# The second half's router and its gate reads earlier, and two more pairs of layer 2 in row halves

## The reference, cut to what matters

```
logits = xt @ Wr + br
top_p, top_idx = top_k(softmax(logits), 2)
weights = top_p / top_p.sum(-1)
h = gelu(einsum('end,edh->enh', xe, W1) + b1)      # 8 experts, 64 -> 256
y = einsum('enh,ehd->end', h, W2) + b2             # 256 -> 64
out = t + sum of the two selected y, times their weights
```

## Time and profile before

| | us |
|---|---|
| time, median of 3 runs | 60.36 (59.89 to 60.62) |
| the profiled execution, its own time | 60.38 |
| its span | 58.5 |
| PE busy in it | 49.7 (85%) |
| DVE busy | 42.3 (72%) |
| ACT busy | 35.2 (60%) |
| POOL busy | 24.9 (42%) |

### The profile page before, as it was taken

One profiled execution on the slowest core, in us unless ns is written; L12 is line 12 of the kernel. 1 busy time (PEld: TensorE's weight loads), 2 busy tenths in 40 slices (PEclk: granted clock), 3 DMA queues, 4 the chain that ended last, 5 costly groups with the idle time before them and its releaser, 6 DMA issues.

```text
span 58.5 us, 1641 instructions
## 1 busy us (share of the span) xinstructions
PE 49.7 (85%) x556; PEld 29.1 (50%) x556; DVE 42.3 (72%) x175; ACT 35.2 (60%) x79; POOL 24.9 (42%) x49
## 2 busy tenths in 40 slices
PE   1997999999789999999999999995499999776420
PEld 0332847887647887654536445362246632052410
DVE  2198689697998988992600999999997409995630
ACT  5501459970958699798896978969708982000000
POOL 6239770000099899765099900298080000026000
PEclk9999999999999999999999999999999999999985
DMA  0351446983000000000000467601559600020012
GB/s 0 105 106 25 113 114 193 349 282 112 1 17 0 0 0 0 11 0 6 0 11 17 126 184 189 210 20 71 195 207 214 207 18 0 29 61 0 0 32 57
DMA packets 4584, 4.80 MB, mean 82 GB/s; under 512 B 2204, under 2 KB 3040, under 8 KB 4576
## 3 DMA queue, kind: packets, MB, share of 16 engines
q1 hardware_dynamic: 4256, 4.67, 26.6%
q10 hardware_dynamic: 320, 0.03, 0.6%
HBM read 4.41 MB, written 0.29 MB: 80 GB/s over the span
## 4 chain that ended last, share of the span: by engine, by line
PE 47%; DVE 16%; DMA 15%; issue 9%; SPq 7%; POOL 1%; ACT 1%; ACTq 0%; DVEq 0%; POOLq 0%
PE banks L1046 13%; PE banks L1074 9%; DMA G<-gates_kept 8%; SPq L312 6%; PE banks L980 4%; PE banks L1027 4%; PE banks L953 3%; DVE HG L746 3%; DMA X<-in_x_dram 3%; PE banks L1116 3%; DMA gates_kept<-gateT 3%; PE banks L932 2%; DVE PTS L602 2%; PE banks L1130 2%; PE banks L916 2%
## 5 line engine op out<-in xcount | busy, mean ns | idle before, releaser
L480 ACT ACTIVATE H<-banks,PF 128x512 f32<-128x512 f32 x32 | 19.6, 685 | 2.1 <-PE banks L1046 1.4
L1046 PE MATMUL banks<-XE,W1F 64*64 64x256 f32 x224 | 14.2, 380 | 0.1
L373 POOL TENSOR_TENSOR acc<-acc,gated 128x512 f32<-128x512 f32 x4 | 5.5, 1386 | 14.3 <-DVE gated L739 8.4
L1046 PEld LDWEIGHTS banks<-XE,W1F 64*64 64x64 f32 x224 | 8.5, 133 | 5.3 <-issue 3.3
L1074 PE MATMUL banks<-H,W2F 64*64 64x512 f32 x80 | 9.6, 594 | 1.5 <-issue 1.5
L356 POOL TENSOR_SCALAR XE<-XF,PF,LB 128x256 f32<-128x256 f32 x14 | 7.7, 564 | 2.2 <-ACT XF L458 2.2
L725 DVE TENSOR_TENSOR YS<-banks,YA 128x512 f32<-128x512 f32 x5 | 3.4, 689 | 4.7 <-ACT YA L490 4.4
L334 POOL TENSOR_TENSOR rs<-base,half 128x2 f32<-128x2 f32 x4 | 2.8, 701 | 8.6 <-DVE base L638 8.4
L916 PE MATMUL banks<-zeros 128*128 128x512 f16 x13 | 5.2, 534 | 1.3 <-POOL zeros L375 1.3
L1074 PEld LDWEIGHTS banks<-H,W2F 64*64 64x64 f32 x80 | 2.9, 132 | 5.2 <-issue 4.8
L490 ACT ACTIVATE YA<-banks,B2T 128x512 f32<-128x512 f32 x5 | 3.4, 687 | 3.1 <-PE banks L1074 3.1
(11 more groups left out here) (93 smaller groups left out, 80.2 us busy)
## 6 DMA issues: line engine op xcount, KB each, us to landing
GS<-gates_kept SPq DMA_DIRECT2D x14, 128.0 KB, 2.9
W1F<-in_w_dram SPq DMA_DIRECT2D x1, 768.0 KB, 4.9
W2F<-in_w_dram SPq DMA_DIRECT2D x1, 512.0 KB, 5.6
G<-gates_kept SPq DMA_DIRECT2D x2, 256.0 KB, 4.1
W1F<-in_w_dram SPq DMA_DIRECT2D x1, 256.0 KB, 3.3
out_dram<-res SPq DMA_DIRECT2D x4, 64.0 KB, 1.6
X<-in_x_dram SPq DMA_DIRECT2D x2, 64.0 KB, 2.0
X<-in_x_dram SPq DMA_DIRECT2D x1, 128.0 KB, 2.4
```

What stands on the lines that cost most here:

```text
L373: nc.gpsimd.tensor_tensor(acc[h][:, :], acc[h][:, :], gated[s % 2][:, :], ALU.add).then_inc(acc_ready, 1)
L480: nc.scalar.activation(H[:, r, :].rearrange("p (t n) -> p t n", t=PT), ps_z[z_slot(g // J)][:, :, PIX * j:PIX * j + PIX], ACT.Gelu, bias=P ...
L1046: mm = nc.tensor.matmul(ps_z[z_slot(q)][C * c:C * c + C, k, PIX * j:PIX * j + PIX], W1F[rows, e, j, C * c:C * c + C], XE[h][rows, e, :], s ...
```

## The change

- `SPLIT` is 7: steps 5 and 6 take the split form too (`layer2` is gone). For each of them a `keep_part` on ACT and a `sum_parts` on DVE are added, and `weigh` reads `YS` and `GS` in place of a bank.
- PE: `turn_gates(0)` and `turn_x2(3)` come ahead of `layer1(5)`; `logits(1)` goes from behind `layer1(7)` to ahead of `layer1(6)`; `turn_gates(1)` from behind `layer1(10)` to behind `layer1(7)`; `layer2_split(5)` comes ahead of `layer1(15)`, and `fold_sum` behind `layer2_split(6)`.
- ACT: `turn_gates(0)` and `turn_x2(3)` come ahead of `gelu(10)`, `tanh(1)` and `turn_gates(1)` further ahead as well.
- DVE: `route(1, 0)` and `route(1, 1)` come ahead of `sum_parts(0)`, all the other stages of `route(1)` ahead of `sum_parts(1)`, both `last_bias` between `sum_parts(1)` and `sum_parts(2)`; near the end `weigh_last(0)` and `(1)` stand ahead of `sum_parts(5)`, and the finish of half 0 stands behind `weigh(6)`.
- SP: the gates of half 1 are written out behind the reads of steps 0 and 1; then come the reads of steps 2 and 3, then those of step 7, and then steps 4 to 6.

```diff
-SPLIT = 5
+SPLIT = 7
 def sums_done(s):
-    return 4 * min(s + 1, SPLIT) + 2 * max(s + 1 - SPLIT, 0)
+    return 4 * (s + 1)
...
+            keep_gates(0)
+            spread_pair(0)
+            spread_pair(1)
+            keep_gates(1)
+            spread_pair(2)
+            spread_pair(3)
+            spread_last()
+            for s in range(PAIRS, STEPS - 1):
+                spread_pair(s)
...  (ACT)
             keep_part(0)
-            gelu(10)
             turn_gates(0)
             turn_x2(3)
-            for g in range(11, 14):
-                gelu(g)
-            keep_part(1)
-            for g in range(14, 17):
+            for g in range(10, 13):
                 gelu(g)
             tanh(1)
-            gelu(17)
+            gelu(13)
+            keep_part(1)
+            gelu(14)
+            turn_gates(1)
+            for g in range(15, 18):
+                gelu(g)
             keep_part(2)
...
-            for g in range(26, HALVES * UNITS):
+            for g in range(26, 30):
                 gelu(g)
+            keep_part(5)
+            gelu(30)
+            gelu(31)
+            keep_part(6)
...  (DVE, sum_parts and weigh)
-                if s == 4:
-                    dve.wait_ge(gated_ready, 1)
+                if s >= 4:
+                    dve.wait_ge(gated_ready, s - 3)
...
-                if s < SPLIT:
-                    dve.wait_ge(ysum_ready, s + 1)
-                    nc.vector.tensor_tensor(dst[:, :], YS[s % 4][:, :], GS[s][:, :], ALU.mult)...
-                else:
-                    dve.wait_ge(y_ps, sums_done(s))
-                    nc.vector.scalar_tensor_tensor(out=dst[:, :], in0=ps_y[s % 2], scalar=B2T[:, p:p + 1],
-                                                   in1=GS[s][:, :], op0=ALU.add, op1=ALU.mult)...
+                dve.wait_ge(ysum_ready, s + 1)
+                nc.vector.tensor_tensor(dst[:, :], YS[s % 4][:, :], GS[s][:, :], ALU.mult)...
...  (DVE, order; route(1, 0) and route(1, 1) ahead)
-            sum_parts(1)
+            sum_parts(0)
             for stage in range(2, 11):
                 route(1, stage)
+            sum_parts(1)
+            last_bias(0)
+            last_bias(1)
             sum_parts(2)
             weigh(0)
             weigh(1)
             weigh(2)
-            last_bias(0)
             sum_parts(3)
             weigh(3)
-            last_bias(1)
             sum_parts(4)
             weigh(4)
             weigh_last(0)
             weigh_last(1)
+            sum_parts(5)
+            weigh(5)
+            weigh_last(2)
+            weigh_last(3)
+            sum_parts(6)
+            weigh(6)
             finish_part()
             finish_first()
-            weigh_last(2)
-            weigh_last(3)
-            weigh(5)
-            weigh(6)
             add_third()
...  (PE, order)
             layer2_split(0)
-            layer1(5)
             turn_gates(0)
             turn_x2(3)
+            layer1(5)
+            logits(1)
             layer1(6)
             layer2_split(1)
             layer1(7)
-            logits(1)
+            turn_gates(1)
             layer1(8)
             layer2_split(2)
             layer1(9)
             layer1(10)
-            turn_gates(1)
             layer2_split(3)
             layer1(11)
             layer1(12)
             layer2_split(4)
             layer1(13)
             layer1(14)
+            layer2_split(5)
+            layer1(15)
+            layer2_split(6)
             fold_sum()
-            layer1(15)
-            layer2(5)
-            layer2(6)
             layer2_last(0)
             layer2_last(1)
```

More of the change, by code:

```diff
@@ L99, in build_block @@
         ps_part = [banks[:, 4 + r, :] for r in range(2)]
-        ps_y = [banks[:, 4 + k, :] for k in range(2)]
         ps_b2 = banks[:, 3, 0:PAIRS]
@@ L298, in _, with keep_gates, spread_pair, spread_last @@
             sp.dma_start(B2R[:, :, :], b2[0, E - 2:E, :].partition_broadcast(P)).then_inc(b2r_in, 16)
-            for s in range(STEPS):
-                h, p = s // PAIRS, s % PAIRS
[L302 to L306, removed]
-                for k in range(2):
-                    if s == STEPS - 1:
-                        sp.dma_start(G7[:, k, :], gates_kept[h, 2 * p + k, :].partition_broadcast(P)).then_inc(g7_in, 16)
-                    else:
-                        sp.dma_start(GS[s][C * k:C * k + C, :], gates_kept[h, 2 * p + k, :].partition_broadcast(C))\
-                            .then_inc(gates_in[s], 16)
+            def keep_gates(h):
+                sp.wait_ge(gateT_ready, h + 1)
+                sp.dma_start(gates_kept[h, :, :].rearrange("e (t n) -> t e n", t=TILES), gateT[h][:, :])\
+                    .then_inc(gates_out[h], 16)
+            def spread_pair(s):
+                h, p = s // PAIRS, s % PAIRS
+                sp.wait_ge(gates_out[h], 16)
+                for k in range(2):
+                    sp.dma_start(GS[s][C * k:C * k + C, :], gates_kept[h, 2 * p + k, :].partition_broadcast(C))\
+                        .then_inc(gates_in[s], 16)
+            def spread_last():
+                sp.wait_ge(gates_out[1], 16)
+                for k in range(2):
+                    sp.dma_start(G7[:, k, :], gates_kept[1, E - 2 + k, :].partition_broadcast(P)).then_inc(g7_in, 16)
+            keep_gates(0)
[7 more added lines that the diff above has]
+                spread_pair(s)
             for n in range(0, TILES, PT):
@@ L527, in _ @@
             keep_part(0)
-            gelu(10)
             turn_gates(0)
             turn_x2(3)
-            for g in range(11, 14):
-                gelu(g)
-            keep_part(1)
-            for g in range(14, 17):
+            for g in range(10, 13):
                 gelu(g)
             tanh(1)
-            gelu(17)
-            keep_part(2)
-            gelu(18)
-            gelu(19)
-            turn_gates(1)
-            gelu(20)
-            gelu(21)
+            gelu(13)
[4 more added lines that the diff above has]
+                gelu(g)
+            keep_part(2)
+            for g in range(18, 22):
+                gelu(g)
             keep_part(3)
@@ L733, in weigh @@
                 dst = acc[h] if p == 0 else gated[s % 2]
-                if s < SPLIT:
-                    dve.wait_ge(ysum_ready, s + 1)
-                    nc.vector.tensor_tensor(dst[:, :], YS[s % 4][:, :], GS[s][:, :], ALU.mult).then_inc(gated_ready, 1)
-                else:
-                    dve.wait_ge(y_ps, sums_done(s))
-                    nc.vector.scalar_tensor_tensor(out=dst[:, :], in0=ps_y[s % 2], scalar=B2T[:, p:p + 1],
-                                                   in1=GS[s][:, :], op0=ALU.add, op1=ALU.mult).then_inc(gated_ready, 1)
+                dve.wait_ge(ysum_ready, s + 1)
+                nc.vector.tensor_tensor(dst[:, :], YS[s % 4][:, :], GS[s][:, :], ALU.mult).then_inc(gated_ready, 1)
             def weigh_last(n):
@@ L881, in _ @@
             second_norm(3)
-            sum_parts(0)
             route(1, 0)
             route(1, 1)
-            sum_parts(1)
+            sum_parts(0)
             for stage in range(2, 11):
                 route(1, stage)
+            sum_parts(1)
+            last_bias(0)
+            last_bias(1)
             sum_parts(2)
@@ L1078, in layer2_split @@
                                 mm.then_inc(y_ps, 1)
[L1080 to L1091, removed]
             def turn_b2():
```

## The result

The change makes the kernel slower: 61.56 us (median of 4 runs, 60.91 to 61.78) against 60.12, a ratio of 1.0245 (95% interval 1.0124 to 1.0367). Run again, unaltered, on another occasion it gave 61.54 against 60.46, ratio 1.0203 (1.0142 to 1.0264). So it is slower; whether by more than 2% the intervals leave open. The forecast of 60.4 with a range to 61.0 was wrong.

A forecast was written before the change was run, and what follows sets the result against it. The prediction took step 7's gate reads, a last_bias/POOL collision and DVE's end as bounds; 1.49 and 0.77 of holes went on about 1.3 of router, 0.9 of idle and a longer tail: 60.38 + 0.06 = 60.4 us, range 59.1 to 61.0.

The forecast's parts named there:

- The path now: Products wait for step 7's reads (0.77 idle); last_bias meets POOL's additions, 1.49 idle ahead of layer2_split(4).
- The gate reads and last_bias: Step 7's DMA wait goes, moved gate writing costs nothing; eight last_bias instructions take 1.7 to 2.2 us, hidden.
- The router: POOL's stretches hold seven two-input DVE instructions; gate ends at 33.0, layer2_split(2) starts at 34.2 (32.89 before).
- The round of the banks: Split layer 2 round of 3.62 us, level with PE's work; PE idles about 0.9 between steps 5 and 6.
- The tail: From layer2_split(6)'s start to add_third 4.98 us, and the 0.73 wait for POOL's add_up(5) goes.
- rival C: At the end add_up(5) on POOL gets in ahead of product 2, rest 0.3 later; 60.8 (60.5 to 61.2), chance 0.13.
- B: Rival: router's small DVE instructions are not caught by POOL's stretches; 59.5 us (59.0 to 59.9), chance 0.22.
- D: Rival: PE's clock falls before L1130, its 1.08 us doubles, 61.5; chance 0.04. Elsewhere D: layer2_split(0)'s start to span's end.
- E: Rival: the holes close further than seen, for instance a round shorter than 3.62; below 59.0 us, chance 0.06.
- The sum: layer2_split(2) at 34.2 puts add_third at 53.66 against 53.60, total 60.38 + 0.06 = 60.4 us.
- The count from 60.38: Starting point: the profiled execution's 60.38 us, taken as equivalent to the median of three runs, 60.36.

The follow-up runs named there:

- g7_first: Kernel before, with SP issuing the two reads of step 7 ahead of those of steps 4 to 6: 59.26 us, ratio 0.9820.
- bias_ahead: Kernel before with step 7's reads ahead of those of steps 4 to 6 and both last_bias between sum_parts(2) and weigh(0): 57.94 us, ratio 0.9680.
- router_off_path: Changed kernel with turn_gates(1) behind layer2_split(2) on PE, keep_part(2) on ACT, sum_parts(1) between stages 7 and 8 of route(1): 61.12 us, ratio 1.0117.
- router_off_reads: router_off_path with SP issuing the reads of steps 2 and 3 ahead of the writing of half 1's gates: 59.90 us, ratio 0.9880.
- stretch_behind: Changed kernel with POOL waiting for half 1's gates before seven of the eight stretches: 59.99 us in a single execution (kernel before 60.24).
- finish_ahead: Changed kernel with fold_sum ahead of layer2_split(6) and the finish of half 0 ahead of weigh_last(2): 61.84 us, ratio 1.0197.

## Why the prediction was wrong, point by point

The forecast failed in three places: two terms of its sum were too small, the router's (by 0.22) and the tail's (by 0.29), and it was counted from one execution that had started early. The points follow its own order.

- **The path now.** Right: g7_first shows the DMA wait (1.34 of D), bias_ahead the collision of `last_bias` (a further 1.20).
- **The gate reads and last_bias.** Right. The products start without a DMA wait, L768 takes 1.86, and there is no idle ahead of `layer2_split(4)`. That moving the writing of the gates ahead of two steps of reads costs "nothing" held only because the gates were early: router_off_path shows 2.45 of wait once they are not.
- **The router.** The mechanism was right, and it is the largest single cost of the front (1.05, router_off_reads and stretch_behind). The term was 0.22 short: `layer2_split(2)` at 9.14, not 8.92. I had counted LG and gate among the caught, which slipped through at 0.19 each, and not the cast (0.50) and wab (0.53 for two), which have one input in SBUF each. wab ends at 33.23, where a stretch ends at 33.21. I had quoted the Trainium skill (SBUF — State Buffer, Who interferes with whom) only in half: its sentence on at most one SBUF input holds outside the two-port modes, and the same section names `copy`, `cast` and `tensor_scalar` among those that can enter such a mode and contend. The trace agrees that they are held, 0.50 beside a stretch and 0.17 without; in which mode they ran no row shows.
- **The round of the banks.** Right: 3.62, 3.65, 3.63, 3.63 against 3.62, and an idle of 0.82 between steps 5 and 6 against 0.9.
- **The tail.** Among the terms of the sum this step failed most: "From S6: 2.06 to `keep_part(6)`, 0.78 to `sum_parts(6)`, 0.61 to `weigh(6)`", in all 4.98. It was 5.27. `weigh(6)` starts 0.81 behind `sum_parts(6)`, not 0.61, because it waits for that very sum's semaphore, where most earlier `weigh` read a sum of some steps ago; in the profile before `sum_parts(3)` at 41.04 has its `weigh(3)` at 41.85, so the 0.81 was there to be read. And product 3, held by `add_up(5)` as rival C says, ended at 52.83 and kept `sum_parts(6)` 0.08 past its due time.
- **Rival C.** Its mechanism came true in part: POOL got in ahead of product 3 and not of product 2, so it cost 0.08 and not 0.3. It was not the main cause.
- **Rivals B, D and E.** B (the router is not caught) did not come: cast, hot, wab and part took 0.50 to 0.61 above. D did not occur: the last fold took 1.08 at a granted clock of 1.00, which fell only after it, between 58.0 and 58.5. E did not either: no round was shorter than 3.62.
- **The sum.** 0.22 in the router, 0.05 in the rounds, 0.29 in the tail: 0.56 together, which is what `add_third` comes later than predicted, counted from the common start.
- **The count from 60.38, and the range.** The failing step is "so I count from either alike". One profile stood for the kernel, and in it `layer2_split(0)` started at 25.28, near the earliest seen (25.2, where the latest is 26.2). The profiled execution after took 61.78 against a sum of 60.44: 0.88 of the difference is its later start, 0.55 is D, and 0.10 less lies outside the span. With D alone right, 33.8 and the starts seen give 60.8 to 61.8, so the range to 61.0 was too narrow as well.
- **What the medians add.** They differ by 1.1 to 1.4, the profiles' D only by 0.6 (33.22) to 0.75 (33.08). An estimate from the spans of all executions bears on the rest. In the other kernels a span less the D of its kernel gives a mean start of 25.7 (54 executions); the kernel before spans 58.6 on average (58 executions), which leaves it a mean D of about 32.9. So the change costs about 0.9 of D against the average of the kernel before, and by this estimate both profiles of it lie at its long end. It takes the starts to be spread alike in all kernels, which no run shows for this one.
- **What the forecast missed as a whole.** The holes that go are worth 1.34 and 1.20 each; the change closed both and paid 2.17 for the split tail and 1.05 for the router: 33.22 - 1.34 - 1.20 + 2.17 + 1.05 = 33.90, measured 33.83. I had set 0.9 and a longer DVE chain of no stated price against the tail, and 1.3 against the router, and had taken the holes at 1.49 and 0.77. The split tail was under-priced: between steps 5 and 6 it has one layer 1 to hide a round made for two (idle 0.82), and DVE must then do a sum, a product and the finish in a row behind the last split layer 2. Of the 2.17, about 0.5 is the place of the finish and of `fold_sum` (0.51 in finish_ahead); the rest was not taken apart.

## What to carry to other kernels

Work that is moved earlier runs beside other work than before: look for what its neighbours on the shared ports will be, instruction by instruction, and not only for what it frees. A form that costs nothing in the steady state of a pipeline (here a round of 3.62 for two layers 1 on PE) costs its whole latency at the end, where nothing is left to run beside it. Before a bundle of reorderings, try each alone: here one loop order on SP gave 1.34 of D, nearly all of the 1.56 that the whole front of the bundle gave, and two moves gave 57.9 us.

## What the runs showed of the hardware that was not expected

- The same matmuls at the start (three of 128x512, float16) take 0.81 to 1.49 us from one execution to the next. The first record of the full granted clock begins at 4.1 to 7.1 us in the fourteen traces, and the whole of the rest shifts with it by up to 1.0 us. Two programs should be compared from an instruction behind that point.
- DVE instructions with one input in SBUF can be held by POOL too: the cast took 0.50 us beside a stretch and 0.17 without, two TENSOR_SCALAR 0.53 and 0.23. `sum_parts`, with one input in PSUM and one in SBUF, took 0.69 beside additions and stretches as without.
- The time outside the span is not constant between programs: 1.75 to 1.92 us in ten of them, 2.42 to 3.12 in the two with `fold_sum` ahead of the last split layer 2.
